# Second cross attention: key strips four a step, and the first score tiles two projections later

## What is computed

```python
x = x + _L0_xattn_ref(_layernorm(x), ctx, ctx, mask, ...)
x = x + _L0_ffn_ref(_layernorm(x), ...)      # self attention and 8 experts
x = x + _L1_xattn_ref(_layernorm(x), ctx, ctx, ...)
x = x + _L1_ffn_ref(_layernorm(x), ...)      # 8 experts that choose tokens
```

```python
query  = _split_heads(q @ Wq + bq)           # 16 heads of 16
key_   = _split_heads(k @ Wk + bk)           # 64 keys for each batch
value  = _split_heads(v @ Wv + bv)
logits = einsum('bhqd,bhkd->bhqk', query, key_) / sqrt(16)
out    = einsum('bhqk,bhkd->bhqd', softmax(logits), value)
return concat(out) @ Wo + bo
```

## Time and profile before

| | |
|---|---|
| median of 3 runs | 1891.6 us (1888.62 to 1894.38) |
| profiled execution | 1894.03 us, span 1892.3 us |
| TensorE busy | 1683.1 us, 89% of the span |
| VectorE, ScalarE, GpSimd busy | 1246.7, 975.4 and 573.0 us |
| start of the second cross attention to its first `transpose_max` | 1388.0 to 1451.3 us, TensorE busy 52.17 of 63.30 us |
| attention loop behind it | 1451.3 to 1582.0 us, TensorE busy 125.37 of 130.70 us |

### The profile page before, as it was taken

The page is one execution under the profiler, slowest core; times in us unless marked ns, Lnnn a source line. Parts: engine busy times, 40 slices in busy tenths (PEclk is TensorE's granted clock), DMA queues, the critical chain, the costliest instruction groups (busy, mean ns, idle before and its releaser), DMA issues. The chain is left out here.

```text
span 1892.3 us, 29292 instructions
## 1 busy us (share of the span) xinstructions
PE 1683.1 (89%) x10227; PEld 790.5 (42%) x10228; DVE 1246.7 (66%) x2177; ACT 975.4 (52%) x1825; POOL 573.0 (30%) x645
## 2 busy tenths in 40 slices
PE   6899799899999999999999796599959997529997
PEld 4566554222222222222222375377635664215555
DVE  7444458788888888888885188488854554681222
ACT  5323155588888888888888431255545332202221
POOL 5200063243221121111221126367745000113433
PEclk9999999899999999999999897799979999759999
DMA  5000069632222222223200432322130000522542
GB/s 150 1 2 1 20 188 314 206 80 41 41 41 41 41 41 41 41 58 57 47 1 2 154 116 83 117 58 66 52 109 1 1 2 1 198 97 53 138 113 34
DMA packets 112865, 134.71 MB, mean 71 GB/s; under 512 B 18672, under 2 KB 88688, under 8 KB 112464
## 3 DMA queue, kind: packets, MB, share of 16 engines
q1 hardware_dynamic: 102016, 114.33, 22.2%
q0 software_dynamic: 9552, 17.97, 4.0%
q10 hardware_dynamic: 1152, 0.54, 0.1%
HBM read 78.60 MB, written 54.06 MB: 70 GB/s over the span
## 5 line engine op out<-in xcount | busy, mean ns | idle before, releaser
L1027 DVE TENSOR_REDUCE sa_mhalf<-sa_a 128x2 f32<-128x1024 f32 x512 | 604.1, 1220 | 83.9 <-PE sa_a L1239 82.0
L1172 ACT ACTIVATE sa_e<-sa_b 128x512 f32<-128x512 f32 x683 | 383.9, 602 | 76.4 <-PE sa_b L1272 76.3
L1282 PE MATMUL sa_b2o<-sa_e,sa_v 128*17 128x512 f32 x2048 | 269.5, 598 | 0.0
L1172 ACT ACTIVATE sa_e<-sa_b2o 128x512 f32<-128x512 f32 x341 | 205.3, 602 | 40.4 <-PE sa_b2o L1272 40.4
L1272 PE MATMUL sa_b<-sa_q,sa_k 112*128 112x512 bf16 x468 | 163.0, 387 | 2.7 <-ACT sa_e L1172 2.7
L975 POOL TENSOR_TENSOR sa_rden<-sa_o_rows,sa_minus_one 128x16 f32<-128x16 f32 x32 | 93.0, 2906 | 178.3 <-ACT sa_o_rows L1155 178.3
L250 DVE TENSOR_REDUCE xa_mx<-xa_rows 128x16 f32<-128x1024 f32 x64 | 78.3, 1224 | 84.3 <-PE xa_rows L557 84.0
L1239 PE MATMUL sa_a<-sa_k,sa_q 48*128 48x512 bf16 x704 | 113.1, 388 | 13.3 <-DVE sa_mhalf L1027 13.2
L964 POOL CAST sa_negm<-sa_neg 16x128 bf16<-16x128 f32 x32 | 9.3, 292 | 348.0 <-issue 339.0
L442 ACT ACTIVATE xa_pT<-xa_cols 128x1024 f32<-128x1024 f32 x64 | 62.1, 1021 | 80.9 <-PE xa_cols L589 80.9
L1272 PEld LDWEIGHTS sa_b<-sa_q,sa_k 112*128 112x128 bf16 x468 | 40.6, 97 | 150.9 <-ACT sa_e L1172 129.3
(11 more groups left out here) (352 smaller groups left out, 2975.8 us busy)
## 6 DMA issues: line engine op xcount, KB each, us to landing
k_parts<-sa_parts SPq DMA_DIRECT2D x96, 128.0 KB, 2.2
tc_w<-in_L_ffn_W SPq DMA_DIRECT2D x24, 512.0 KB
sa_q<-q_parts SPq DMA_DIRECT2D x44, 192.0 KB, 5.4
sa_k<-k_parts SPq DMA_DIRECT2D x44, 192.0 KB, 5.7
q_parts<-sa_parts SPq DMA_DIRECT2D x16, 384.0 KB, 3.4
ex_xg<-expert_in SPq DMA_DIRECT2D x39, 132.0 KB, 2.1
v_groups<-sp_vt SPq DMA_DIRECT2D x8, 544.0 KB, 4.5
sa_v<-v_groups SPq DMA_DIRECT2D x16, 272.0 KB, 7.4
```

The costliest lines, as they stand in the source:

```text
L1027: nc.vector.tensor_reduce(mhalf[a % 2][:, half, head:head + PAIRED + 1:PAIRED, t], aps[a_slot(use)][:], axis=X, op=ALU.max).then_inc(a_use ...
L1172: nc.scalar.activation(ex[(KT * n + kt) % (LAG + 1)][:, head], bps[use % 3], ACT.Exp, scale=SCALE).then_inc(b_used, 1)
L1282: last = nc.tensor.matmul(ops[32 * head:32 * head + VW], vs[s][:, kt, head], ex[(KT * n + kt) % (LAG + 1)][:, head], start=(kt == 0), stop ...
```

## The change

ScalarE's `place_keys` calls are spread: four strips at each of the steps 2 to 5, behind `evacuate_xnT` and `normalize_rows` of the step, in place of eight at steps 3 and 4 in front of them. The waits for the key bias and for both halves of the key projection move to step 2. On TensorE the four `scores(0, t)` go behind `project_q(4)` to `project_q(7)`, in place of `project_q(2)` to `project_q(5)`, and the wait for the sixteen strips stands behind `project_q(3)`, in place of `project_q(1)`. The wait for `qT_ready` ahead of the scores is dropped (`project_q(1)` and later ones wait for it already). The programs of VectorE, GpSimd and SyncE are the same.

```diff
                 if not masked:
                     for step in range(CHUNKS + 3):
-                        if step == 3:
-                            act.wait_ge(kbias_made, 1)
-                        if 3 <= step < 5:
-                            act.wait_ge(k_psum, step - 2)
-                            for h in range(HH):
-                                place_keys(step - 3, h)
                         if 2 <= step < CHUNKS + 2:
                             evacuate_xnT(step - 2)
                         if 1 <= step < CHUNKS + 1:
                             normalize_rows(step - 1)
+                        if step == 2:
+                            act.wait_ge(kbias_made, 1)
+                            act.wait_ge(k_psum, HALVES)
+                        if 2 <= step < 6:
+                            for n in range(4 * (step - 2), 4 * (step - 1)):
+                                place_keys(n // HH, n % HH)
                         if step >= 3:
                             for half in range(HALVES):
                                 evacuate_qT(step - 3, half)
...
                         project_q(c)
-                        if c == 1:
+                        if c == CT - 1:
                             pe.wait_ge(kblk_made, H)
-                        if 2 <= c < CT + 2:
-                            pe.wait_ge(qT_ready, HALVES)
-                            scores(0, c - 2)
+                        if c >= CT:
+                            scores(0, c - CT)
```

## The result

| | before | after |
|---|---|---|
| median | 1894.4 us (1888.6 to 1894.7, 5 runs) | 1911.7 us (1904.1 to 1913.5, 5 runs) |
| span of the profiled execution | 1892.3 us | 1905.6 us |
| T(1) to M | 46.64 us | 61.78 us |

The ratio is 1.009, with a 95% interval of 1.0076 to 1.0105: slower by 0.9%, 17.3 us in the medians and 13.3 in the two spans. T(1) to M runs from the second transpose of the stretch (1404.64 before) to the first `transpose_max` (1451.28). It is the part that the change touches, without what differs between executions ahead of it, and it grew by 15.1 us.

A forecast was written before the change was run, and what follows sets the result against it. The start of the stretch was taken as bound by ScalarE and its order, the rest by TensorE. Terms -4.28 + 6.82 + 3.97 + 1.1 + 3.22 + 3.15 = +14.0 us on 1891.6 gave 1905.6 us, range 1899 to 1912.

The forecast's parts named there:

- T(5) earlier: On TensorE, `transpose_xn(5)` comes at about 1427.22 instead of 1431.50 us, with ScalarE's strips spread four a step: -4.28 us.
- stop ahead of T(6): TensorE's `transpose_xn(6)` waits for VectorE's `make_x_shift(6)`, queued behind the maximum of `scores(0, 0)`: 7.89 us in place of 1.07, +6.82.
- stop ahead of T(7), with the copy beside the adds: `transpose_xn(7)` waits for `make_x_shift(7)` behind the maximum of `scores(0, 1)`, +3.97 us; VectorE's copy stretched by GpSimd's adds, +1.1.
- two cold starts: TensorE restarts at the lower clock after both new stops, 1.61 us each: +3.22 us.
- S(2) and the tail, T(7) to M: From `transpose_xn(7)` to the first `transpose_max`, with two score tiles and the last maximum and copy: 11.87 us against 8.72, +3.15.
- The early gain: Start of the stretch: spread strips remove the 3.17 us wait and low clock at `transpose_xn(3)`; `transpose_xn(5)` 4.28 us earlier.
- The chain over VectorE: In-order VectorE makes shifts 6 and 7 only after maxima of new score tiles, delaying the next transposes: +6.82 and +3.97 us.
- The copy beside the bias adds: VectorE's copy of the maxima in the second chain meets GpSimd's eight adds: cost 0 to 2.16 us, taken as +1.1.
- The rival of warm restarts: TensorE's stops come as computed but its clock never falls: +10.8 us, 1902.4 us; chance 0.15.
- The rival of deeper stops: 2.7 us for each of TensorE's cold starts and 2.16 for VectorE's copy: +17.3 us, 1908.9 us; chance 0.13.
- The rival in which VectorE does not hold T(6): `make_x_shift(6)` and (7) pass before `scores(0, 0)` lands, so no stops: -1.1 us, 1890.5 us; chance 0.05.

The follow-up runs named there:

- e1: Kernel before with only ScalarE's half of the change (four strips a step), score tiles still behind projections 2 to 5; ratio 0.9986.
- e3: Changed kernel with VectorE's maxima one step later; ratio 1.0017 to the kernel before.
- e5: Changed kernel with its score tiles one projection earlier (behind 3 to 6), VectorE's order untouched; one execution, 1896.3 us.
- e2: Kernel before with only TensorE's half of the change (score tiles behind projections 4 to 7), strips still eight a step; ratio 1.0091.
- e9: Changed kernel with 7 and 6 extra matmuls of 512 columns, needed by no result, in TensorE's two stops; one execution, 1909.5 us.
- e7: Changed kernel with GpSimd's eight bias adds held until the four maxima of chunk 0 are copied; one execution, 1912.7 us.
- e8: Changed kernel with VectorE's maxima one step later and GpSimd's bias adds held until the last shift is made; ratio 0.9998 to the kernel before.

## Why the prediction was right

The time, 1911.7 us, fell within the range (1899 to 1912), 0.3 us under its upper end, and the sign and mechanism were as forecast. That it stayed inside is in part luck. Of the 6.1 us above the forecast of 1905.6, 2.8 come from the kernel before, whose median was 1894.4 in this comparison and 1891.6 in the profile that the forecast started from; the other 3.3 are the difference of the medians, 17.3 in place of 14.0. Term by term, T(1) to M:

| term | forecast | measured |
|---|---|---|
| T(5) earlier | -4.28 | -4.17 |
| stop ahead of T(6) | +6.82 | +6.72 |
| stop ahead of T(7), with the copy beside the adds | +3.97 + 1.1 = +5.07 | +6.36 |
| two cold starts | +3.22 | +1.43 + 1.60 = +3.03 |
| S(2) and the tail, T(7) to M | +3.15 | +3.23 |
| sum | +14.0 | +15.1 |

The measured terms come from the timeline: T(1) to T(5) 22.69 us against 26.86; S(0) to T(6) 7.79 and S(1) to T(7) 7.43, each less 1.07; T(6) to S(1) 5.89 and T(7) to S(2) 6.06, each less 4.46; T(7) to M 13.57, less its cold start, against 8.74. They add up to 15.17, and 0.04 is gained between T(5) and S(0).

- *The early gain* is right in its steps: T(3) without its wait, two waits of 1.29 us where 1.3 was given, and the full clock. e1 shows it alone: T(3) is 11.03 us behind T(1) there, as in the changed kernel, and was 14.19 before.
- *The chain over VectorE* is right to 0.1 us at T(6). The second stop was said to be 4 to 6 us and was 6.30, by the term below. That the order is its cause is shown from two sides: e3 changes nothing but the order and the first stop is gone, e5 leaves the order and gives VectorE more time.
- *The copy beside the bias adds* is the term that was mis-sized. I priced a chance for one operation. Copy and shift both stand in the chain and both can be held; the second, which I had taken at 0.15 us, was 2.31. Measured +1.3 over the forecast in the changed kernel, and the shift took 2.3 in e2, e3 and e9 too. e7 shows it away with the adds. The first cross attention of the profile before could not show it, as the masked call makes no shift there, but the section "Who interferes with whom" of the Trainium skill's page "SBUF — State Buffer" names it: a VectorE instruction with two SBUF inputs contends with a GpSimd instruction that reads SBUF. The trace agrees: `make_x_shift` reads `mv` and `rstd`, took 2.31 us, and its end falls on the end of an add. That sentence does not cover the copy, which has one input and was held all the same (1.32 us in e2, 2.13 in e3, 1.97 in e9). I had priced the copy alone.
- *The clock.* Two cold starts were right, and their price within 0.2 us. The rival of warm restarts, and with it the reading that a handoff to VectorE costs no clock, is refuted for a stop of this length: granted clock 0.50 behind both stops in the changed kernel. The Trainium skill, page "TensorE: Matmul & The Clock Gate", section "Loop structure matters more than you think", from which I drew that rival, speaks of matmuls that follow at once, and these followed 6.7 us later; it was my reading that went too far. e9 shows that work in the stop keeps it at 1.00. The price is not a constant: T(6) to S(1) took 5.89, 7.25 and 7.39 us in three kernels with the same stop of 6.7 us, so a cold start was worth 1.4 to 2.9 us. The rival of deeper stops gave 2.7 us for each and +17.3 in all. That is just the difference of the medians, but not what the profiled execution shows, where the two were 1.43 and 1.60.
- *The rest of the gap.* The forecast was 14.0 us over the kernel before. The stretch accounts for 15.1 in the profiled execution, the medians differ by 17.3. The changed kernel's profiled execution (1907.4 us) is 4.3 under its median, and the 5 us that it gained behind M, by an earlier full clock and in the routing, are no part of the change. Its slower executions also have the lower mean clock: 0.945 at 1904.1 us, 0.943 at 1907.4, 0.941 in the three from 1911.7 to 1913.5. Longer restarts behind the stops, as in e2 and e7, would do that too. There is no trace of these executions, so how the last 2 us divide between the part behind M and the restarts stays open.

The rival in which VectorE does not hold T(6) was said to end at -1.1 us. e8, which makes it true, ended at -0.06, and 0.92 us of the difference are the last copy's: the tail was taken free of the adds, and in that kernel it isn't.

## What to carry to other kernels

When work is moved on one engine, look at the engine that consumes it: if its program is in order and has the consumer in front of work that the producer needs next, a later producer turns slack into a round trip. The price can be read from the trace before, as the time from the producer to each instruction queued behind the consumer. Here the same edit with the score tiles one projection earlier cost 15.6 us less, so count the steps of slack that each placement leaves.

## What the hardware showed that was not expected

- A VectorE operation on 128x4 elements (0.13 to 0.16 us alone) took 2.31 or 2.32 us beside a GpSimd add of 128x1024, and ended with it. The copy of 128x128 (0.23 alone) took 0.53 to 2.43 us, also ending with an add: what counted was where in the add the operation arrived. The maxima (L250), which read PSUM, took 1.21 to 1.23 us with the adds beside them and without.
- The clock fell for a short wait: in e3 the wait ahead of T(7) was 2.39 us and in e9 2.40 us. In e9 T(7) itself was at the lower clock. In e3 T(7) ran at full speed, and the clock fell during the projection behind it, which took 5.29 us for 3.60, in the table by stretch:

```profile
1440.00:1442.00 2.00, 0.84 (x8) 0.84 (x9) 1.33 (x2) 2.00 (x5) 2.00 (x2) 1.00 0.00 0
1442.00:1444.00 2.00, 2.00 (x6) 0.95 (x5) 0.00 (x0) 1.28 (x2) 2.00 (x2) 0.62 0.00 0
1444.00:1446.00 2.00, 2.00 (x4) 0.73 (x3) 0.00 (x0) 0.63 (x1) 2.00 (x2) 0.53 0.00 0
1446.00:1448.00 2.00, 2.00 (x10) 0.96 (x10) 0.00 (x0) 0.64 (x2) 2.00 (x1) 1.00 0.00 0
```

PEclk is the third column from the end, 1.00, 0.62, 0.53 and 1.00. A wait of 1.14 us in e5 and those of 1.29 us ahead of Q(2) and Q(3) left it at full speed.

- The length of a wait does not settle it. The wait of 1.31 us ahead of the sixteen matmuls of L626, shown with the result, is the same in all eleven traces. In six of them the matmuls took 3.72 us, in the five others (before, e2, e5, e7 and e8) 5.16 to 5.41. In the first stretch, waits of 3.18 to 3.47 us ahead of T(0) left the clock up, and the 3.07 us ahead of T(1) had the low clock behind them in every trace.
